# A two-layer graph aggregation on one core: the layers' steps of four blocks moved later and further apart, and a ring of 14 groups of gathered rows instead of 8

## The reference, cut to what matters

```python
src, dst = (edge_index[0], edge_index[1])
h = _gin_agg(x, src, dst, eps1, n)     # (1 + eps1) * x + segment_sum(x[src], dst)
h = jax.nn.relu(h @ W1a + b1a)         # 256 -> 512
h = jax.nn.relu(h @ W1b + b1b)         # 512 -> 512
h = _gin_agg(h, src, dst, eps2, n)     # second aggregation, next stage of the kernel
h = jax.nn.relu(h @ W2a + b2a)         # 512 -> 512
out = h @ W2b + b2b
```

## Time and profile before

| | us |
|---|---|
| median of the runs | 4545.82 (4534.95, 4545.82, 4551.21) |
| span of the profiled execution | 4526.2 |
| PE busy | 3407.3 (75%) |
| POOL busy | 2794.2 (62%) |
| DVE busy | 1481.5 (33%) |
| ACT busy | 497.8 (11%) |
| first aggregation, first to last start of a gather | 71.5 to 1284.7 |
| first gather of the second aggregation | 1333.4 |

### The profile page before, as it was taken

One profiled execution on the slowest core, in us unless ns is written; L12 is line 12 of the kernel. 1 busy time (PEld: TensorE's weight loads), 2 busy tenths in 40 slices (PEclk: granted clock), 3 DMA queues, 4 the chain that ended last, 5 costly groups with the idle time before them and its releaser, 6 DMA issues. The chain is left out here.

```text
span 4526.2 us, 40559 instructions
## 1 busy us (share of the span) xinstructions
PE 3407.3 (75%) x12357; PEld 2256.3 (50%) x12359; DVE 1481.5 (33%) x5707; ACT 497.8 (11%) x1161; POOL 2794.2 (62%) x2815
## 2 busy tenths in 40 slices
PE   3577777878878889899999976566556656658997
PEld 2354444545453444444444455345444444438986
DVE  5112121212121433444333445234343343442221
ACT  4010000000110000000000002000000000003432
POOL 4666666666646666666666502666666666635664
PEclk7788888988889999999999987777777778769998
DMA  6333333433349666666666527334334333327887
GB/s 199 90 112 112 111 110 110 131 111 111 109 128 330 194 198 200 193 190 194 195 201 205 170 104 240 108 114 123 115 117 128 115 114 114 119 80 174 203 210 188
DMA packets 321341, 687.10 MB, mean 152 GB/s; under 512 B 58976, under 2 KB 148300, under 8 KB 320854
## 3 DMA queue, kind: packets, MB, share of 16 engines
q0 software_dynamic: 169712, 474.01, 37.9%
q10 hardware_dynamic: 86448, 110.35, 7.4%
q1 hardware_dynamic: 64970, 100.14, 6.8%
HBM read 592.43 MB, written 99.13 MB: 153 GB/s over the span
## 5 line engine op out<-in xcount | busy, mean ns | idle before, releaser
L280 POOL DMA_INDIRECT s_edge_rows<-table,w_src_idx x2538 | 2495.4, 983 | 1235.3 <-issue 712.6
L320 PE MATMUL s_psA<-s_edge_rows,s_onehot 128*128 128x257 f32 (+2 forms) x4932 | 1695.0, 487 | 212.1 <-DMA s_edge_rows<-table,w_src_idx 92.3
L320 PEld LDWEIGHTS s_psA<-s_edge_rows,s_onehot 128*128 128x128 f32 x4932 | 1012.6, 210 | 758.6 <-issue 635.1
L295 DVE TENSOR_SCALAR s_onehot<-w_iota_row,w_dst_l 128x128 f32<-128x128 bf16 x2466 | 531.6, 296 | 28.5 <-PEq L149 16.4
L2031 POOL DMA_INDIRECT acc_rows<-s_y,s_tnode x105 | 166.3, 1584 | 130.7 <-DVE s_y L2154 98.8
L1011 PE MATMUL s_psM<-s_h1T,s_w1b 128*128 128x512 f32 (+2 forms) x448 | 195.2, 582 | 52.5 <-ACT s_h1T L913 49.0
L330 PE MATMUL s_psA<-s_edge_rows,s_early 128*128 128x257 f32 (+2 forms) x648 | 221.3, 468 | 10.2 <-issue 9.0
L1017 PE MATMUL s_psM<-s_w2a,s_hT 128*128 128x512 f32 x392 | 196.3, 647 | 22.7 <-issue 16.6
L2179 PE MATMUL s_psU<-s_xT,s_w 128*128 128x128 f32 x1680 | 208.2, 278 | 0.2 <-ACT s_xT L2085 0.2
L2179 PEld LDWEIGHTS s_psU<-s_xT,s_w 128*128 128x128 f32 x1680 | 199.3, 195 | 0.6 <-issue 0.6
L2189 PE MATMUL s_psD<-moe_w,s_hT 128*128 x840 | 199.5, 381 | 0.0
(11 more groups left out here) (364 smaller groups left out, 2802.6 us busy)
## 6 DMA issues: line engine op xcount, KB each, us to landing
s_w<-in_L_ffn_W_dram SPq DMA_DIRECT2D x105, 512.0 KB
s_edge_rows<-table,w_src_idx POOLq DMA_INDIRECT x2538
s_swT<-swt_rows SPq DMA_DIRECT2D x12, 1024.0 KB
table<-s_trow ACTq DMA_DIRECT2D x11, 1024.0 KB
own_rows<-s_own ACTq DMA_DIRECT2D x11, 1024.0 KB
s_self_h<-own_rows ACTq DMA_DIRECT2D x11, 1024.0 KB
swt_rows<-s_swT ACTq DMA_DIRECT2D x11, 1024.0 KB
extra_rows<-w_zeros SPq DMA_DIRECT2D x7, 896.0 KB
```

Of the source, the lines that this page charges most:

```text
L280: pool.indirect_dma_start(self.rows[:, g % self.SLOTS, t, :], None, self.table, bass.IndirectOffsetOnAxis(ap=src_idx[:, at:at + 1], axis=0 ...
L295: last = nc.vector.tensor_scalar(into[:, t, :], iota_row[:, q * P:(q + 1) * P], dst_l[:, at + t:at + t + 1], None, ALU.is_equal)
L320: last = nc.tensor.matmul(banks[b % 2][:, 0:w], self.onehot[:, g % self.AHEAD, t, :], self.rows[:, g % self.SLOTS, t, col:col + w], start= ...
```

## The change

The first aggregation gets a ring of 14 groups (`slots=14`); the two other aggregations keep 6. The step numbers become FIRST 1 to 4, SECOND 7, 9, 11, 13, THIRD 17, 19, 21, 23, store 24. Steps are spread from turn 4 on instead of turn 2 (`first=4`); steps 22 to 24 fall into the first steps of the super after (`late`), and close stands behind group 3 of the next block on PE and ACT (`close_at=3`); on DVE it stays ahead of group 0.

The turns, for a super of four blocks whose steps are made during the next one (a turn is the group after which the step stands; 4' and 5' are turns of the super after that):

| | FIRST | SECOND | THIRD | store | close on PE and ACT |
|---|---|---|---|---|---|
| before | 2, 2, 3, 4 | 6, 8, 10, 12 | 15, 17, 19, 21 | 22 | 1, 7, 13, 19 |
| after | 4, 5, 6, 7 | 10, 11, 13, 15 | 18, 20, 22, 4' | 5' | 3, 9, 15, 21 |

```diff
-        def pipeline(group, close, piece, begin=None, close_first=False):
+        def pipeline(group, close, piece, begin=None, close_first=False, late=0, close_at=1, first=2):
+
+            def pieces(s, k):
+                if 0 <= s < len(SUPER):
+                    piece(s, k)
+                if 0 <= s - 1 < len(SUPER) and k < late:
+                    piece(s - 1, STEPS + k)
...
-                    if g == 1 and b and not close_first:
+                    if g == close_at and b and not close_first:
                         close(b - 1)
                     for k in range(STEPS):
-                        if s and i == 2 + k * (len(turns) - 2) // STEPS:
-                            piece(s - 1, k)
+                        if s and i == first + k * (len(turns) - first) // STEPS:
+                            pieces(s - 1, k)
             close(NB - 1)
             for k in range(STEPS):
-                piece(len(SUPER) - 1, k)
+                pieces(len(SUPER) - 1, k)
+            for k in range(late):
+                pieces(len(SUPER), k)
...
-            FIRST, SECOND, THIRD = (0, 1, 2, 3), (5, 7, 9, 11), (14, 16, 18, 20)
-            edges = Edges(S, table1, T1_W, ((0, D + 1),), FP32, GPB - 1)
+            FIRST, SECOND, THIRD, STORED = (1, 2, 3, 4), (7, 9, 11, 13), (17, 19, 21, 23), 24
+            LATE_STEPS = STORED + 1 - STEPS
+            edges = Edges(S, table1, T1_W, ((0, D + 1),), FP32, GPB - 1, slots=14)
...
-                    if k == STEPS - 1:
+                    if k == STORED:
...
-                pipeline(lambda b, g: None, close, piece)
+                pipeline(lambda b, g: None, close, piece, late=LATE_STEPS, close_at=3, first=4)
...
-                pipeline(group, close, piece, close_first=True)
+                pipeline(group, close, piece, close_first=True, late=LATE_STEPS, first=4)
...
-                pipeline(group, close, piece)
+                pipeline(group, close, piece, late=LATE_STEPS, close_at=3, first=4)
```

## The result

The changed kernel takes 4581.81 us (median, 4576.85 to 4591.74) where the kernel before takes 4543.1 us in the same comparison: ratio 1.0082, 95% interval [1.0063, 1.0102]. It is **slower** by 38.7 us, 0.8%; 4486 us were forecast. The profiled execution took 4591.74 us for a span of 4589.9, so 1.8 us lie around a span. The 19.6 us that I put between span and median were a difference between executions. The two profiled executions are thus a poor pair: their spans (4526.2 and 4589.9) lie 63.7 us apart, the medians 38.7. What follows tells where time was lost, not how much of it. Four single executions stand far outside their comparisons and are in no ratio: 4560.84 us at a granted clock of 0.726, and 11,866, 13,139 and 14,526 us.

A forecast was written before the change was run, and what follows sets the result against it. It took POOL's and PE's waits on late news in the first aggregation as the bound, no engine being full. -75 us (ring and spacing) +15 (stage end) = -60 us, 4526.2 to 4466, plus 19.6 gives 4486 us; range 4425 to 4560.

The forecast's parts named there:

- The ring: First aggregation: 14 slots instead of 8 cut POOL's stops to 22, gaining 59 us; with step spacing 75 us.
- the straight line from the earlier trace: First aggregation: low end for 14 slots, carried on from the third aggregation's 6 and the first's 8: 42 stops, gain 8 us.
- The end of the stage: After the first aggregation's last gather: POOL up to six groups further ahead, PE finishes later; +15 us, bounds 0 and 17.
- Steps further apart: The first aggregation's block closes and ACT's relu: half of 20 PE waits go, 63 us idle; 16 us credited.
- The news waits for POOL's pause: First aggregation: PE's reports pass only when gathers pause; ten remaining waits each 11.4 us longer, +51 us, 4597 us; chance 0.17.
- Ring and steps were not the limit: First aggregation: stops grow longer as they get fewer; gain 8 us or less, given back at end; 4546 us; chance 0.19.
- POOL at its own pace: First aggregation: all 138 us of POOL's stops go, less 17 at the end: -121 us, 4425 us; chance 0.16.
- The page's rule: First aggregation: repeated gaps on POOL can mean too few buffers, so all 138 us would go; the forecast took 75.

The follow-up runs named there:

- ring14_third: Kernel before with only the first aggregation's ring deepened to 14 slots, steps unmoved: 4546.08 us against 4518.77, ratio 1.0054.
- steps_third: Kernel before with only the moved steps, ring left at 8 slots: 4540.49 us against 4518.77, ratio 1.0047.
- change_third: The whole change again, ring of 14 and moved steps, against the kernel before at 4518.77 us: 4552.81 us, ratio 1.0074.
- close_early: Kernel before with moved steps and 8 slots, but close kept behind group 1 and FIRST at turns 4, 4, 5, 6: 4090.59 us, ratio 1.0022.
- before_again: The unchanged kernel before, traced again in a comparison where PE's reports came promptly: 4086.71 us.

## Why the prediction was wrong

**The ring, the term that failed.** I took "a stop comes once the free slots are used up, about every 7 groups" and carried it to 14 slots: -59 us and, with the spacing, -75. Measured, ring alone: +4.8 us in the gathers. The number of stops didn't follow the slots: 65 waits with 8, 74 in ring14_third, 65 in the changed kernel. Nor does the straight line from the earlier trace rows (8 us) describe it. The kernel's own rows had a warning in them: one stop every 7 groups would be 40 stops with 8 slots, not 65, and POOL stops with PE's groups done by the records. So it isn't a shortage of slots as such that the stops show, but reports of PE that come late whatever the depth. More slots let PE fall further behind (9 to 12 groups in place of 3 to 8) and leave the stops as many as they were.

**The end of the stage** was a right mechanism: +15 taken with bounds 0 and 17 for the ring, +17.1 measured. That the size fits is partly luck, since I had six groups more left to PE and the records show under four (22 records of L320) and 6 records of L330. The moved steps add 5.1 (late) or 6.8 us (prompt) that I costed at nothing: no cover is left for them there.

**Steps further apart.** The closes and the relu behaved as worked out and better: whatever releaser is named, 158 us of waits (I had counted 126.0), afterwards 26 in the changed kernel's trace, 45 in steps_third and 57 in change_third. What I left out is the next hand-over: from the close's transposes by way of ACT's copy to FIRST, with one group between them as before (turns 1 and 2, now 3 and 4). As long as PE had waited for DVE ahead of the transposes, news was through by then. Now the transposes find the sum ready and FIRST waits for the copy, 131 us where 30 stood. In steps_third each of FIRST's nine longest waits (5.5 to 19.0 us) ends 0.1 us after ACT's copy, which itself starts 9 to 20 us after the transposes' end. I listed FIRST's distances to SECOND and to the bank it needs, not to the step just ahead of it. Of PE's 210 us of waits at the steps 181 are left. That this makes the 13.9 us in the gathers is not shown: close_early met the other condition, and between the four late traces with the steps the gathers vary from 1217.2 to 1230.4 us, about as much.

**The rivals.** "The news waits for POOL's pause" gave 4597 us against 4581.81; its side and its first instance are right: PE's first wait grew by 24.2 us, for the 22.7 that it allowed, and its sign, waits of PE of 20 us and more, came (52.0 and 29.3 us). But its sum isn't. It has every remaining wait 11.4 us longer, and the ring alone leaves them as they were, beside the 78.1 and 13.3 of the earlier trace rows:

```profile
PE s_psT L990 <- DVE s_agg L962: 79.4, 15, 13.0
```

By the lags above the ring stays nearly full all along; it fills once, at the start, and the lag is paid once, at the end. "Ring and steps were not the limit" is right of the ring in the prompt condition and of nothing else. "POOL at its own pace" exists, but no change here brings it about.

**The page's rule.** By the Trainium skill (Perfetto Trace Analysis, Identifying Performance Opportunities) repeated gaps can mean too few buffers; the sum took 75 us of the 138 that it would give. Here it doesn't hold: 8 slots to 14 left 65 gaps in place, and in the prompt condition 5 slots are enough.

**The range** reached to 4560 because I held the slower rival to be 17 in 100. The evidence for it, a release 4 us after POOL's last gather, was weighed against a copy at 785.14 us that came at once; both are true, and one prompt report doesn't refute reports that can be late.

What stays open: what holds PE's reports back, whether a pause of POOL lets them through or only comes with them, and why the same kernel meets this in one comparison and not in the next (the chips differ, as said). The late traces also hold far fewer events of semaphores (22,177 in the kernel before, 56,814 in before_again), which is why so many of their waits are labelled issue or remote; whether that belongs to the cause or follows from it can't be told from them.

## What to carry to other kernels

Before a ring is deepened, ask whether its consumer's groups are really unfinished when the producer stops. If they are done by the records and only unheard of, more slots let the producer run ahead, and the consumer's backlog at the barrier is the price: here 17 us for six slots. Of a step that is moved, list the distance to every neighbour on both sides, the one just ahead of it first. Repeat the kernel before in each comparison, and note the chip: the effect was 0.7 to 0.8% in one condition and 0.2% in the other.

## What the runs showed of the hardware

The unchanged kernel takes 4084 to 4089 us in four comparisons and 4519 and 4543 in two, 10% more, at one and the same 2538 gathers. In the longer executions POOL's gathers keep their 0.96 us and their 0.30 us of distance; what is longer is the way of PE's reports, up to 50.7 us for one (spare sum done at 100.85 us, DVE's read at 151.52), in a window in which DVE was idle. Reports of ACT to DVE stay prompt in the same traces, 0.11 us at most. Each comparison was of one kind, the four single executions aside. TensorE's granted clock goes with it: 0.86 to 0.87 over the kernel in the late condition, 0.93 to 0.94 in the prompt one. A wait for the rows of a gather just issued costs POOL 2.0 us (95 us for 47).
